# Eight output projection tiles moved into the last head, and the last head's copy, inversion and transfers split in halves over two issuing engines

## The chip, the core and the metric

The kernel runs on one core of one Trainium2 chip. The metric is device time in microseconds (us). Three executions of the kernel before took 399.95, 400.23 and 400.28 us, median 400.23. The profile is that of one further execution.

## What is computed

One transformer layer on 2048 tokens of 256 values, in f32: a layer norm, attention with 16 heads of 16 values, in which a query sees 717 of the 2048 keys (the first 205 and the last 512), and a mixture of eight experts of which each token uses one. Cut to what matters here:

```
xn = layernorm(x)
q, k, v = rope(xn Wq + bq), rope(xn Wk + bk), xn Wv + bv       # 16 heads of 16
attn = softmax(q k^T / 4 over the 717 kept keys)
out  = (attn v).reshape(2048, 256)
y    = x + (out Wo + bo) + weight * down_e(silu(gate_e(xn)) * up_e(xn))
```

The change touches only the last head and the product `out Wo`.

## The kernel before

The program is written out by hand, engine by engine, with semaphores between the engines. After layer norm, projections and experts come the 16 heads. In a head, TensorE makes 24 score units (`S`): for each of six chunks of keys (128, 77, 128, 128, 128, 128) and each of four blocks of 512 queries one bank of PSUM is filled, by four matmuls of 32 columns side by side (line 725, three for the chunk of 77). The banks 4, 5 and 6 take turns, so that unit u waits until ScalarE has finished the exponential of unit u-3. ScalarE takes each unit through the exponential (line 1297). When the four units of a chunk are through, TensorE multiplies them with v (`P`, line 703, four matmuls of 32 columns, f32), accumulating in bank 7. Between them TensorE makes in each head sixteen tiles of the next heads' row maxima (`M`, line 646), which VectorE reduces out of the banks 0 to 3. The string `ORDER` sets how S, M and P follow each other. In the last head (h = 15) there are no further heads, and its sixteen places `M` are empty.

The tail. The heads' outputs go as rows to DRAM, and come back as `attnT`, 128 rows (heads 0 to 7, m = 0) and 128 rows (heads 8 to 15, m = 1); the softmax sums take the same way, are inverted, and come back as `recips`. VectorE multiplies the two (`divide`, line 1131). Heads 0 to 7 are divided before the last head is half done; heads 8 to 13 near its end. Head 15 skips DRAM: ScalarE copies bank 7 to `o_st` (line 1288), SyncE issues four transfers of its rows to `attnT` (line 415), VectorE inverts the whole copy, sums and all, into `last_recip` (line 1151), SyncE issues four transfers of the inverted sums to `recips` (line 419), and VectorE makes four multiplications for the 32 rows of heads 14 and 15.

The output projection (line 762) has 16 tiles of 128 tokens, each the sum of an m = 0 and an m = 1 matmul of 256 columns. It uses all eight banks, two tiles each. TensorE makes all sixteen with m = 0 and then all sixteen with m = 1. After each pair VectorE adds the residual (line 1161), and SyncE stores 256 KB (line 425). A queue stands behind each engine's program order: SyncE's DMAs are issued one after another, and what waits holds what follows.

## Time and profile before

| | us |
|---|---|
| median of three runs | 400.23 |
| the profiled execution | 404.71 |
| its span, first to last instruction | 402.9 |
| TensorE busy | 372.3 |
| VectorE busy | 322.7 |
| ScalarE busy | 270.1 |

The span is 1.8 us shorter than the profiled execution's own time. Start times in what follows are counted from the start of the span. In the timeline, instructions of one line that follow each other are merged into one row: the second number is the time from the first one's start to the last one's end, and the number in brackets is idle time of the engine before the row, with what ended it. The row of an f32 matmul counts two records for each instruction of the program.

### The profile page before, as it was taken

Reading aid. Unit: us, or ns where it says so; the run is one execution under the profiler, and the core shown is the slowest. Engines: PE = TensorE matmul, PEld = TensorE weight load, DVE = VectorE, ACT = ScalarE, POOL = GpSimd, SP = SyncE. Lnnn points to the kernel's source line nnn. Section 1 sums busy time; section 2 is a strip of 40 time slices with the busy share of each in tenths; the row PEclk is TensorE's granted clock in tenths of the full one; section 3 lists DMA queues with packets and bytes.
Section 4 is the critical chain, followed back from the end, with each engine's and each line's share of the span. In section 5 each row is a group of like instructions: output and inputs, shape, how many; then the busy total and the mean of one; then the engine's idle time right before and its main releaser. Section 6 shows DMA issues by size and latency. Waiting matters only on the chain.

```text
span 402.9 us, 12243 instructions
## 1 busy us (share of the span) xinstructions
PE 372.3 (92%) x4646; PEld 193.2 (48%) x4646; DVE 322.7 (80%) x549; ACT 270.1 (67%) x537; POOL 63.9 (16%) x82
## 2 busy tenths in 40 slices
PE   0889988898999999999999999999999999998896
PEld 0556555565674544444444443444444444542265
DVE  5859598777766888888898888988898888984566
ACT  2614564544445887787877878778887888888920
POOL 5005242332200030321303213030000000000000
PEclk9999998999999999999999999999999999999999
DMA  7999346544513030321303213032021121255726
GB/s 234 407 419 174 113 125 205 166 137 139 132 42 95 15 96 5 97 55 45 91 10 98 58 40 96 8 93 55 19 70 42 33 65 27 52 154 104 144 52 209
DMA packets 30920, 42.53 MB, mean 106 GB/s; under 512 B 10724, under 2 KB 25700, under 8 KB 30048
## 3 DMA queue, kind: packets, MB, share of 16 engines
q1 hardware_dynamic: 29000, 36.71, 31.7%
q0 software_dynamic: 1872, 5.11, 4.9%
q8 instruction: 37, 0.61, 0.6%
q14 instruction: 11, 0.09, 0.1%
HBM read 27.75 MB, written 13.67 MB: 103 GB/s over the span
## 4 chain that ended last, share of the span: by engine, by line
PE 80%; DVE 10%; issue 4%; ACT 3%; DMA 1%; SPq 0%; DVEq 0%; ACTq 0%
PE ps L725 20%; PE ps L703 18%; PE ps L646 18%; PE ps L594 6%; PE ps L607 4%; PE ps L762 3%; PE ps L545 3%; DVE mx L1013 3%; PE ps L632 1%; DMA x_sb<-x_in 1%; PE ps L534 1%; PE ps L507 1%; PE ps L501 1%; PE ps L580 1%; PE ps L653 1%
## 5 line engine op out<-in xcount | busy, mean ns | idle before, releaser
L1013 DVE TENSOR_REDUCE mx<-ps 128x1 f32<-128x717 f32 x232 | 198.6, 899 | 30.9 <-PE ps L646 30.7
L725 PE MATMUL ps<-q_op,k_op 98*32 98x512 bf16 (+1 forms) x1472 | 128.8, 381 | 2.5 <-ACT wqk L1297 0.7
L1297 ACT ACTIVATE probs<-ps 128x512 f32<-128x512 f32 x192 | 103.1, 598 | 18.2 <-PE ps L725 16.5
L646 PE MATMUL ps<-k_op,q_op 96*32 96x512 bf16 (+1 forms) x1856 | 111.1, 315 | 0.4 <-DVE mx L1013 0.3
L646 PEld LDWEIGHTS ps<-k_op,q_op 96*32 96x32 bf16 x1856 | 50.6, 96 | 56.2 <-issue 25.7
L725 PEld LDWEIGHTS ps<-q_op,k_op 98*32 98x32 bf16 (+1 forms) x1472 | 42.0, 95 | 65.5 <-ACT probs L1297 14.9
L703 PE MATMUL ps<-probs,v_op 128*32 128x512 f32 x384 | 50.6, 595 | 0.2 <-ACT o_st L1288 0.2
L1297 ACT ACTIVATE dn<-ps 77x512 f32<-77x512 f32 x64 | 34.8, 595 | 10.9 <-PE ps L725 10.9
L1297 ACT ACTIVATE gu<-ps 128x512 f32<-128x512 f32 x64 | 34.5, 598 | 9.1 <-PE ps L725 9.1
L1297 ACT ACTIVATE wqk<-ps 128x512 f32<-128x512 f32 x64 | 33.5, 599 | 8.1 <-PE ps L725 8.1
L454 POOL COPY v_op<-v_all 128x192 f32<-128x192 f32 x16 | 5.7, 361 | 199.4 <-PE ps L703 199.4
L448 POOL DMA_INDIRECT o_st<-sorted_rows,token_of x23 | 25.1, 1089 | 75.4 <-PE ps L580 46.9
L594 PE MATMUL ps<-gu,probs 128*128 x92 | 32.4, 476 | 4.7 <-ACT probs L1227 4.7
L1007 DVE TENSOR_REDUCE mx<-ps 128x1 f32<-128x717 f32 x24 | 21.7, 903 | 6.7 <-PE ps L632 6.4
L594 PEld LDWEIGHTS ps<-gu,probs 128*128 128x128 f32 x92 | 16.1, 193 | 11.9 <-issue 7.2
L545 PE MATMUL ps<-xnT,wqk 128*128 128x512 f32 (+1 forms) x48 | 19.7, 550 | 0.0
L1045 DVE SCALAR_TENSOR_TENSOR probs<-probs,ps 128x176 f32<-128x176 f32 x23 | 7.6, 330 | 13.2 <-ACT probs L1246 13.2
L703 PE MATMUL ps<-dn,v_op 77*32 77x512 f32 x128 | 17.0, 591 | 0.0
L703 PE MATMUL ps<-gu,v_op 128*32 128x512 f32 x128 | 16.5, 592 | 0.2 <-ACT gu L1297 0.2
L703 PE MATMUL ps<-wqk,v_op 128*32 128x512 f32 x128 | 16.5, 592 | 0.0
L501 PE MATMUL ps<-const,xn 128*128 128x128 f32 x32 | 5.9, 353 | 11.2 <-DVE xn L813 11.2
L1246 ACT ACTIVATE probs<-ps 128x176 f32<-128x176 f32 x23 | 7.2, 315 | 13.3 <-PE ps L594 13.3
(127 smaller groups left out, 377.7 us busy)
## 6 DMA issues: line engine op xcount, KB each, us to landing
q_parts<-parts SPq DMA_DIRECT2D x12, 256.0 KB
sorted_results<-ys SPq DMA_DIRECT2D x23, 128.0 KB
q_op<-q_parts SPq DMA_DIRECT2D x15, 192.0 KB
gu<-gu_in SPq DMA_DIRECT2D x1, 2816.0 KB
tab<-tab_in SPq DMA_DIRECT2D x1, 2048.0 KB, 11.8
sorted_rows<-xn SPq DMA_DIRECT2D x4, 512.0 KB, 7.4
out<-x_sb SPq DMA_DIRECT2D x8, 256.0 KB, 2.4
q_op<-q_parts SPq DMA_DIRECT2D x15, 128.0 KB
```

The source lines that it names most:

```text
L448: pool.indirect_dma_start(out=xs[t % XR], out_offset=None, in_=xn_dram, in_offset=bass.IndirectOffsetOnAxis(ap=token_of[:, t:t + 1], axis= ...
L501: ins = pe.transpose(bank(b)[:, 256 * m + P * j:256 * m + P * j + P], xn[:, 2 * pair + j, P * m:P * m + P], ident)
L545: ins = pe.matmul(proj_bank(u, odd), wqk[:, is_q, HID * m + P * odd:HID * m + P * odd + P], xnT[:, m, t0:t0 + n], start=m == 0, stop=m == ...
L594: ins = pe.matmul(bank(b)[:, 0:2 * I], xsT[b][:, P * m:P * m + P], gu[:, bass.ds(e * (HC * 2 * I) + 2 * I * m, 2 * I)], start=m == 0, stop ...
L607: ins = pe.matmul(bank(4 + b)[:, 0:HID], hidT[b][:, P * m:P * m + P], dn[:, bass.ds(e * (2 * HID) + HID * m, HID)], start=m == 0, stop=m == 1)
L646: ins = pe.matmul(ps[r:r + CW, at + c0:at + c0 + n], q_op[slot][0:KR, P * t + r:P * t + r + CW], k_op[slot][0:KR, c0:c0 + n], start=True, ...
L703: ins = pe.matmul(bank(7)[VW * b:VW * b + VW, :], v_op[slot][0:rows, VW * c:VW * c + VW], prob[c][0:rows, QB * b:QB * b + QB], start=c == ...
L725: ins = pe.matmul(bank(4 + u % RING)[r:r + w, :], k_op[k][:, c0 + r:c0 + r + w], q_op[k][:, QB * b:QB * b + QB], start=True, stop=True)
L762: ins = pe.matmul(ps[:, HID * t:HID * t + HID], attnT[:, m, P * t:P * t + P], wo[:, HID * m:HID * m + HID], start=m == 0 and t % 2 == 0, s ...
L1007: dve.tensor_reduce(mx[:, h, t:t + 1], ps[:, EARLY_MAX:EARLY_MAX + NK], AX.X, ALU.max).then_inc(max_reduced, 1)
L1013: dve.tensor_reduce(mx[:, slot, t:t + 1], ps[:, at:at + NK], AX.X, ALU.max).then_inc(max_reduced, 1)
L1297: act.activation(prob[c][0:rows, QB * b:QB * b + QB], bank(4 + u % RING)[0:rows, :], ACT.Exp, scale=SCALE).then_inc(exp_done, 1)
```

## The change

Four things are moved or split.

1. The m = 0 matmuls of the first eight output tiles (t = 0 to 7) go into the last head, at its places `M` number 6 to 13 (counted from 0). There each is cut into four matmuls of 32 columns, side by side.
2. ScalarE copies bank 7 in two halves of 256 columns, and VectorE inverts each half on its own.
3. ScalarE itself issues the four transfers of the head's rows, and the four transfers of the second half's inverted sums; SyncE issues the four of the first half's.
4. The divisions of heads 14 and 15 are eight of 256 columns. The pairs of output tiles are taken in the order 0, 2, 4, 6, 1, 3, 5, 7 (`PAIRS`), first halves of the four query blocks first; the last four divisions stand between VectorE's first additions.

```diff
+EARLY_OUT = 4 * 2
+OUT_SLOTS = {6 + n: n for n in range(EARLY_OUT)}
+PAIRS = [2 * b + half for half in range(2) for b in range(NQB)]
...
+        def load_last_recip(engine, half, b):
+            c0 = QB // 2 * half
+            engine.dma_start(recips[P - DH:P, HC - 1, QB * b + c0:QB * b + c0 + QB // 2],
+                             last_recip[VW * b + DH:VW * b + 2 * DH, c0:c0 + QB // 2]
+                             ).then_inc(last_recip_in[NQB * half + b], 16)
...
-            sp.wait_ge(o_copied, HEADS)
-            for b in range(NQB):
-                sp.dma_start(attnT[P - DH:P, HC - 1, QB * b:QB * b + QB],
-                             o_st[0][VW * b:VW * b + DH, :]).then_inc(last_in[b], 16)
             sp.wait_ge(last_inverted, 1)
             for b in range(NQB):
-                sp.dma_start(recips[P - DH:P, HC - 1, QB * b:QB * b + QB],
-                             last_recip[VW * b + DH:VW * b + 2 * DH, :]).then_inc(last_in[b], 16)
+                load_last_recip(sp, 0, b)
...
+                        if h == HEADS - 1 and j in OUT_SLOTS:
+                            if OUT_SLOTS[j] == 0:
+                                pe.wait_ge(wo_in, 16)
+                                pe.wait_ge(neg_copied, HEADS)
+                                pe.wait_ge(max_reduced, HEADS * NT)
+                            for r in range(0, P, CW):
+                                out_tile(OUT_SLOTS[j], 0, r, CW)
...
+            pe.wait_ge(exp_done, HEADS * UNITS)
+            for t in range(EARLY_OUT, NT):
+                if t == NT - 2:
+                    pe.wait_ge(last_copied, 2)
+                out_tile(t, 0)
+            for n, pair in enumerate(PAIRS):
+                pe.wait_ge(attn_ready, NQB + n + 1)
+                for t in (2 * pair, 2 * pair + 1):
+                    ins = out_tile(t, 1)
+                ins.then_inc(out_proj, 1)
...
-            dve.reciprocal(last_recip[:], o_st[0][:]).then_inc(last_inverted, 1)
+            for half in range(2):
+                dve.wait_ge(last_copied, half + 1)
+                cols = slice(QB // 2 * half, QB // 2 * half + QB // 2)
+                dve.reciprocal(last_recip[:, cols], o_st[0][:, cols]).then_inc(last_inverted, 1)
             dve.wait_ge(attn_in[2], 32)
-            for b in range(NQB):
-                dve.wait_ge(last_in[b], 32)
-                divide(1, P - 2 * DH, P, b, attn_ready)
             dve.wait_ge(y_added, NT)
...
+            for n in range(NQB):
+                divide_last(n)
+            for n, pair in enumerate(PAIRS):
+                if n < NQB:
+                    divide_last(NQB + n)
+                dve.wait_ge(out_proj, n + 1)
                 both = x_sb[:, 2 * pair:2 * pair + 2, :].rearrange("p t d -> p (t d)")
                 dve.tensor_tensor(both, bank(pair), both, ALU.add).then_inc(out_ready, 1)
...
-            copy_o(HEADS - 1, 0)
+            act.wait_ge(pv_done, HEADS * NCH)
+            act.wait_ge(o_stored, (HEADS - 1) * (16 * NQB))
+            for half in range(2):
+                cols = slice(QB // 2 * half, QB // 2 * half + QB // 2)
+                act.copy(o_st[0][:, cols], bank(7)[:, cols]).then_inc(last_copied, 1)
+            act.wait_ge(last_copied, 2)
+            for b in range(NQB):
+                act.dma_start(attnT[P - DH:P, HC - 1, QB * b:QB * b + QB],
+                              o_st[0][VW * b:VW * b + DH, :]).then_inc(last_o_in[b], 16)
+            act.wait_ge(last_inverted, 2)
+            for b in range(NQB):
+                load_last_recip(act, 1, b)
```

TensorE's program in the last head before, from its product of the second chunk with v (`dn,v_op`) to the output projection (`wo,xnT`):

```order
L703 MATMUL ps<-probs,v_op 32x512 x4
L725 MATMUL ps<-q_op,k_op 32x512 x12
L703 MATMUL ps<-dn,v_op 32x512 x4
L725 MATMUL ps<-q_op,k_op 32x512 x20
L703 MATMUL ps<-probs,v_op 32x512 x4
L725 MATMUL ps<-q_op,k_op 32x512 x16
L703 MATMUL ps<-probs,v_op 32x512 x4
L725 MATMUL ps<-q_op,k_op 32x512 x16
L703 MATMUL ps<-wqk,v_op 32x512 x4
L703 MATMUL ps<-gu,v_op 32x512 x4
L762 MATMUL ps<-wo,xnT 128x256 x32
```

The same place in the changed kernel, from the first moved tiles on (line 718 is the output tile, 739 the score units, 710 the product with v):

```order
L739 MATMUL ps<-q_op,k_op 32x512 x4
L718 MATMUL ps<-wo,xnT 32x256 x8
L739 MATMUL ps<-q_op,k_op 32x512 x8
L710 MATMUL ps<-dn,v_op 32x512 x4
L739 MATMUL ps<-q_op,k_op 32x512 x4
L718 MATMUL ps<-wo,xnT 32x256 x4
L739 MATMUL ps<-q_op,k_op 32x512 x4
L718 MATMUL ps<-wo,xnT 32x256 x4
L739 MATMUL ps<-q_op,k_op 32x512 x12
L718 MATMUL ps<-wo,xnT 32x256 x4
L710 MATMUL ps<-probs,v_op 32x512 x4
L718 MATMUL ps<-wo,xnT 32x256 x4
```

Two tiles now stand between the ninth and the tenth score unit, two between the units of the next group, and one on each side of a product with v; after these rows there are one more between score units, and one ahead of the next product. 24 full-width matmuls are left at the end, of 32.

VectorE's last instructions before (line 1151 inverts, 1131 divides, 1161 adds the residual; in brackets the semaphores that each waits for):

```order
L1151 RECIPROCAL o_st<-o_st 128x512 [waits o_stored,o_copied]
L1131 TENSOR_TENSOR xnT<-xnT,tab 32x512 [waits last_in0,attn_in2]
L1131 TENSOR_TENSOR xnT<-xnT,tab 32x512 [waits last_in1]
L1131 TENSOR_TENSOR xnT<-xnT,tab 32x512 [waits last_in2]
L1131 TENSOR_TENSOR xnT<-xnT,tab 32x512 [waits last_in3]
L1161 TENSOR_TENSOR x_sb<-ps,x_sb 128x512 [waits out_proj,y_added]
L1161 TENSOR_TENSOR x_sb<-ps,x_sb 128x512 [waits out_proj] x7
```

And in the changed kernel, from the first division on (1174 divides, 1184 adds):

```order
L1174 TENSOR_TENSOR xnT<-xnT,tab 32x256 [waits last_o_in0,last_recip_in0,y_added,attn_in2]
L1174 TENSOR_TENSOR xnT<-xnT,tab 32x256 [waits last_recip_in1,last_o_in1]
L1174 TENSOR_TENSOR xnT<-xnT,tab 32x256 [waits last_recip_in2,last_o_in2]
L1174 TENSOR_TENSOR xnT<-xnT,tab 32x256 [waits last_recip_in3,last_o_in3]
L1174 TENSOR_TENSOR xnT<-xnT,tab 32x256 [waits last_recip_in4,last_o_in0]
L1184 TENSOR_TENSOR x_sb<-ps,x_sb 128x512 [waits out_proj]
L1174 TENSOR_TENSOR xnT<-xnT,tab 32x256 [waits last_recip_in5,last_o_in1]
L1184 TENSOR_TENSOR x_sb<-ps,x_sb 128x512 [waits out_proj]
L1174 TENSOR_TENSOR xnT<-xnT,tab 32x256 [waits last_recip_in6,last_o_in2]
L1184 TENSOR_TENSOR x_sb<-ps,x_sb 128x512 [waits out_proj]
L1174 TENSOR_TENSOR xnT<-xnT,tab 32x256 [waits last_recip_in7,last_o_in3]
L1184 TENSOR_TENSOR x_sb<-ps,x_sb 128x512 [waits out_proj] x5
```

There are now five divisions ahead of the first addition, and one ahead of each of the next three.

## Rows read from the trace of the kernel before

**Rows 1.** The page: busy time, share of the span and instructions of two engines

```profile
PE 372.3 (92%) x4646; PEld 193.2 (48%) x4646; DVE 322.7 (80%) x549; ACT 270.1 (67%) x537; POOL 63.9 (16%) x82
```

**Rows 2.** Chain of waits, 370 to 403 us: start us, us, what

```profile
381.18 0.86 PE ps L703 x8
...
384.49 1.07 PE ps L703 x8
385.56 14.03 PE ps L762 x64
...
399.61 0.69 DVE x_sb L1161
```

**Rows 3.** Timeline of TensorE's matmuls in the last head: start us, us, instructions

```profile
370.56 0.83 PE L725 MATMUL ps<-q_op,k_op 98*32 98x512 bf16 x12
...
375.36 0.91 PE L725 MATMUL ps<-q_op,k_op 98*32 98x512 bf16 x12
376.10 1.03 PE L703 MATMUL ps<-dn,v_op 77*32 77x512 f32 x8
...
378.77 1.03 PE L703 MATMUL ps<-probs,v_op 128*32 128x512 f32 x8
...
380.78 0.40 PE L725 MATMUL ps<-q_op,k_op 98*32 98x512 bf16 x4 [0.33 <-ACT wqk L1297]
381.01 1.03 PE L703 MATMUL ps<-probs,v_op 128*32 128x512 f32 x8
381.87 0.82 PE L725 MATMUL ps<-q_op,k_op 98*32 98x512 bf16 x12
```

**Rows 4.** Timeline of ScalarE, last head

```profile
382.37 2.06 ACT L1297 ACTIVATE gu<-ps 128x512 f32<-128x512 f32 x4 [0.18 <-PE ps L725]
```

**Rows 5.** Timeline of all engines, the tail

```profile
385.62 0.58 ACT L1288 COPY o_st<-ps 128x512 f32<-128x512 f32 x1 [1.19 <-PE ps L703]
386.24 2.48 SPq L415 DMA_DIRECT2D xnT<-o_st  x4
386.24 3.35 DVE L1151 RECIPROCAL o_st<-o_st 128x512 f32<-128x512 f32 x1 [0.99 <-ACT o_st L1288]
389.62 2.41 SPq L419 DMA_DIRECT2D tab<-o_st  x4
391.63 2.51 DVE L1131 TENSOR_TENSOR xnT<-xnT,tab 32x512 f32<-32x512 f32 x4 [2.03 <-DMA tab<-o_st]
394.17 2.68 DVE L1161 TENSOR_TENSOR x_sb<-ps,x_sb 128x512 f32<-128x512 f32 x4
394.89 5.81 SPq L425 DMA_DIRECT2D out<-x_sb  x8
```

**Rows 6.** Groups of instructions by line and form: busy us, mean ns, idle before

```profile
L762 PE MATMUL ps<-wo,xnT 128*128 128x256 f32 x64 | 14.1, 381 | 0.0
L1260 ACT COPY ys<-ps 128x256 f32<-128x256 f32 x23 | 8.6, 375 | 10.7 <-PE ps L607 9.2 <-issue 1.5
L1102 DVE RECIPROCAL recip_c<-sum_c 128x16 f32<-128x16 f32 x15 | 3.7, 244 | 9.2 <-DMA sum_c<-softmax_sums 9.2
L980 DVE TENSOR_TENSOR v_all<-ps,bvo 128x256 f32<-128x256 f32 x5 | 1.8, 412 | 0.0
```

**Rows 7.** Busy time in stretches: us, engines, granted clock, DMA share, GB/s

```profile
395.00:396.00 1.00, 1.00 (x7) 0.87 (x6) 1.00 (x2) 0.00 (x0) 0.00 (x0) 1.00 0.14 48
396.00:397.00 1.00, 1.00 (x6) 0.90 (x5) 0.74 (x2) 0.00 (x0) 0.00 (x0) 1.00 1.05 339
...
401.00:402.00 1.00, 0.00 (x0) 0.00 (x0) 0.00 (x0) 0.00 (x0) 0.00 (x0) 1.00 0.97 330
402.00:403.00 1.00, 0.00 (x0) 0.00 (x0) 0.00 (x0) 0.00 (x0) 0.00 (x0) 0.68 0.04 11
```

**Rows 8.** Line 419, its DMAs, from issue to landing

```profile
DMA to landing us min/median/max: 1.9/2.0/2.0
```

**Rows 9.** Line 425, the stores of the output, from issue to landing

```profile
DMA to landing us min/median/max: 2.2/2.4/2.6
```

More of the change, by code:

```diff
@@ L228, in layer @@
         attn_in = [sem(f"attn_in{n}") for n in range(3)]
-        last_in = [sem(f"last_in{b}") for b in range(NQB)]
+        last_copied = sem("last_copied")
+        last_o_in = [sem(f"last_o_in{b}") for b in range(NQB)]
+        last_recip_in = [sem(f"last_recip_in{n}") for n in range(2 * NQB)]
         last_inverted = sem("last_inverted")
@@ L411, in _ @@
             load_attn(HEADS - 2, HEADS - 1, attn_in[2])
-            sp.wait_ge(o_copied, HEADS)
-            for b in range(NQB):
-                sp.dma_start(attnT[P - DH:P, HC - 1, QB * b:QB * b + QB],
-                             o_st[0][VW * b:VW * b + DH, :]).then_inc(last_in[b], 16)
             sp.wait_ge(last_inverted, 1)
             for b in range(NQB):
-                sp.dma_start(recips[P - DH:P, HC - 1, QB * b:QB * b + QB],
-                             last_recip[VW * b + DH:VW * b + 2 * DH, :]).then_inc(last_in[b], 16)
+                load_last_recip(sp, 0, b)
             ov = out_d.rearrange("(t p) d -> p t d", p=P)
-            for pair in range(NT // 2):
-                sp.wait_ge(out_ready, pair + 1)
+            for n, pair in enumerate(PAIRS):
+                sp.wait_ge(out_ready, n + 1)
                 sp.dma_start(ov[:, 2 * pair:2 * pair + 2, :], x_sb[:, 2 * pair:2 * pair + 2, :]
@@ L706, in pv, with out_tile @@
                 ins.then_inc(pv_done, 1)
+            def out_tile(t, m, r=0, w=P):
+                pe.wait_ge(attn_ready, NQB if m else t // 4 + 1)
+                return pe.matmul(ps[r:r + w, HID * t:HID * t + HID], attnT[:, m, P * t + r:P * t + r + w],
+                                 wo[:, HID * m:HID * m + HID], start=m == 0 and t % 2 == 0,
+                                 stop=m == HC - 1, skip_group_check=True)
             def head_step(h, k, first=False, rest_of_next=True, start_after=True):
@@ L755, in _ @@
             pv(15, NCH - 1, 0)
-            def out_tile(t, m):
-                pe.wait_ge(attn_ready, NQB * m + t // 4 + 1)
-                ins = pe.matmul(ps[:, HID * t:HID * t + HID], attnT[:, m, P * t:P * t + P],
-                                wo[:, HID * m:HID * m + HID], start=m == 0 and t % 2 == 0,
-                                stop=m == HC - 1, skip_group_check=True)
-                if m == HC - 1 and t % 2 == 1:
-                    ins.then_inc(out_proj, 1)
-            pe.wait_ge(wo_in, 16)
-            pe.wait_ge(neg_copied, HEADS)
-            for m in range(HC):
-                for t in range(NT):
-                    if m == 0 and t == NT // 2:
-                        pe.wait_ge(exp_done, HEADS * UNITS)
-                        pe.wait_ge(o_copied, HEADS)
-                    out_tile(t, m)
+            pe.wait_ge(exp_done, HEADS * UNITS)
[8 more added lines that the diff above has]
+                ins.then_inc(out_proj, 1)
         @block.vector
@@ L1148, in _, with divide_last @@
                 divide(1, 0, P - 2 * DH, b)
-            dve.wait_ge(o_copied, HEADS)
             dve.wait_ge(o_stored, 16 * NQB * (HEADS - 2))
-            dve.reciprocal(last_recip[:], o_st[0][:]).then_inc(last_inverted, 1)
+            for half in range(2):
+                dve.wait_ge(last_copied, half + 1)
+                cols = slice(QB // 2 * half, QB // 2 * half + QB // 2)
+                dve.reciprocal(last_recip[:, cols], o_st[0][:, cols]).then_inc(last_inverted, 1)
             dve.wait_ge(attn_in[2], 32)
-            for b in range(NQB):
-                dve.wait_ge(last_in[b], 32)
-                divide(1, P - 2 * DH, P, b, attn_ready)
             dve.wait_ge(y_added, NT)
-            for pair in range(NT // 2):
-                dve.wait_ge(out_proj, pair + 1)
+            rows = slice(P - 2 * DH, P)
+            def divide_last(n):
+                dve.wait_ge(last_o_in[n % NQB], 16)
+                dve.wait_ge(last_recip_in[n], 16)
+                cols = slice(2 * P * PAIRS[n], 2 * P * PAIRS[n] + 2 * P)
+                dve.tensor_tensor(attnT[rows, 1, cols], attnT[rows, 1, cols], recips[rows, 1, cols], ALU.mult
+                                  ).then_inc(attn_ready, 1)
+            for n in range(NQB):
+                divide_last(n)
+            for n, pair in enumerate(PAIRS):
+                if n < NQB:
+                    divide_last(NQB + n)
+                dve.wait_ge(out_proj, n + 1)
                 both = x_sb[:, 2 * pair:2 * pair + 2, :].rearrange("p t d -> p (t d)")
```

## The prediction

> **What bounds the kernel now.** I read the page first: TensorE is busy for 92% of the span, ScalarE for 67% [rows 1]. Those are averages over stages, and the change touches only the last head and the tail, so I went to the chain of waits from 370 us on. It has two parts. In the last head it goes to and fro between TensorE and ScalarE; a product with v at 381.18 is one of its pieces [rows 2], and the timelines show each of the two waiting for the other, TensorE 0.33 us for an exponential at 380.78, ScalarE 0.18 for a score unit at 382.37 [rows 3, 4]. From 384.49 us on it is TensorE alone: the last product with v, 64 records of the output projection without a gap until 399.6, and one addition [rows 2]. The last head's transfers are not in that chain: the divisions run from 391.63 to 394.14 [rows 5], and TensorE reaches the m = 1 tiles at about 385.6 + 32 x 0.217 = 392.5, when the first of them is done.
>
> The view of stretches shows a second bound at the same place. From 396 to 402 us the DMA engines are full, at 330 to 340 GB/s; the 0.14 in the stretch before puts their start at 395.9, and the next to nothing in the last one their end at 402.05 [rows 7]. Eight stores of 262 KB took 6.15 us, 0.77 each. So the end of the kernel is the larger of two: the first store's data plus 6.15, and the last store's issue plus its own way. The last store is issued when the addition that starts at 399.61 ends (400.3), and lands 2.2 to 2.6 us later [rows 2, 9]. Both give 402.1 for the last byte. Whoever wants to gain in the tail must start the first stores earlier and not leave gaps between them.
>
> **Step 1: eight tiles in the last head.** An m = 0 tile is two records. 64 records take 14.03 us, and one lasts 0.38 [rows 2, 6], so they follow each other after (14.03 - 0.38) / 63 = 0.217 us, and a tile costs 0.43 us. No row shows its new form, four quarters of 32 x 256 in f32. The nearest one is the product with v, four quarters of 32 x 512 in f32: from 381.01 to 381.87, 0.86 us [rows 3]; with half the columns 0.43. From below: the bf16 score unit, four quarters, (0.82 - 0.38) / 2 = 0.22 us [rows 3], if a quarter needed one pass; from above 0.86, if the quarters shared nothing of the shorter length. I take 0.43, since the product with v has the same type, the same width and two passes.
>
> So 8 x 0.43 = 3.46 us leave the tail and enter the head. What hides them there is TensorE's idle time. The first moved tile stands behind the score unit that starts at 375.36, the last one ahead of the product that starts at 381.01 [rows 3]. From 375.36 to 381.87, 6.51 us, TensorE does twelve score units (12 x 0.22 = 2.6) and three products with v (3 x 0.86 = 2.6) [rows 3]. 1.3 us are idle. At least 3.46 - 1.3 = 2.1 us cannot be hidden, and ScalarE has little slack: the score unit at 381.87 lets its exponential start at 382.37, 0.50 later, and ScalarE had already been idle for 0.18 [rows 3, 4].
>
> How much of the 1.3 us is used I worked out by walking the program: each score unit starts when TensorE is free and 0.05 us after the exponential three units back has ended; an exponential starts 0.50 after its unit or 0.48 to 0.49 after the one before, and lasts 0.60; three of the four gaps in 2.06 us give (2.06 - 0.60) / 3 = 0.49 [rows 4]. Without the tiles the walk hits every start in rows 3 within 0.06 us. With them TensorE is idle twice for 0.08 before the unit that was at 381.87, which moves to 384.1. After it nothing is moved, and the rest of the head keeps its shape. The last product with v goes from 384.49 to 386.74: D = 2.25 us. With 0.22 us for a tile the same walk gives D = 1.0, with 0.50 it gives 2.65, with 0.86 it gives 5.5. The three tiles that stand directly before or after a product with v (places 10, 11, 13) cost their whole 0.43 each; only those between score units that wait for ScalarE (9 and 12) cost nothing alone.
>
> **Step 2: copy and inversion in halves.** Times from here are in the frame of before; D is added at the end. The copy starts at 385.62. Half of it is 0.375 us (a copy of 256 columns, rows 6) instead of 0.58. The reciprocal of 16 columns takes 0.244 and that of 512 takes 3.35 [rows 5, 6], 6.26 ns a column, so 256 take 1.75 us. The first half starts at 386.03 and ends at 387.78, where before the whole ended at 389.59: 1.8 us earlier.
>
> **Step 3: transfers.** SyncE issues its four at 387.8. Four issues take 2.41 us [rows 5], 0.6 us apart, and each lands 1.9 to 2.0 later [rows 8]. I keep both for the half-size transfers; from below an issue could cost half, 0.3. They land at 389.75, 390.3, 390.95 and 391.55. ScalarE's rows are issued from about 386.3, if it issues as SyncE does; they land by 390.2 and have 1.4 us to spare. Its second halves are issued at about 389.5, land from 391.45 and have 0.5 us to spare. No row shows ScalarE issuing a DMA; that is bounded by nothing (if it issues faster) and by the 0.6 us of SyncE's issue added to each of its own four if the two queues share what issues them, 2.4 us.
>
> Four issues in a row take longer (2.41 us) than one transfer takes to land (2.0) [rows 5, 8]. The Trainium skill, DMA: Bandwidth & Descriptors, section "Issuing engines are not separate DMA queues", says that issuing from several engines saves only the issue time, "which is usually small relative to the DMA itself". By that rule the split over two engines would be worth next to nothing; by the rows it is not small here, since four further issues on SyncE would have ended at 388.8, after the first half's inversion at 387.8, and the split is worth 1.0 us. The sum goes by the rows.
>
> **Step 4: VectorE.** A division of 512 columns follows the one before after 0.61 us, (2.51 - 0.68) / 3 [rows 5]. One of 256 costs between 0.31 (half) and 0.41 (a tensor_tensor of 256 columns, rows 6); I take 0.34. An addition behind a division starts only when that has ended: 391.63 + 2.51 = 394.14, and the addition at 394.17 [rows 5], so there a switch costs 0.1 more. Divisions 0 to 3 follow the transfers, the last at 391.63; division 4 at 391.97; the first addition at 392.35, its store 0.72 later (394.17 to 394.89, rows 5) at 393.07. Before it was 394.89: 1.8 us earlier. But then an addition with a division ahead of it comes only every 0.61 + 0.34 = 0.95 us, or 1.05 with the switch, while a store needs 0.77 us. The first three gaps leave the DMA engines idle for 3 x 0.18 to 3 x 0.28, 0.55 to 0.85 us, and then the stores run at 0.77. What is left of 1.8 is 0.95 to 1.25 us; I take 1.1. TensorE is no bound there: from 390.3 it makes a pair in 0.86 and would be through at 397.2.
>
> **The sum.** D - 1.1 = 2.25 - 1.1 = +1.15 us. The profiled execution would go from 404.71 (span 402.9 and 1.8 around it) to 405.9. The median of the runs is 4.5 us below the profiled one; I carry the difference over: 400.23 + 1.15 = 401.4 us. The forecast's own range is 400.9 to 401.9, for D between 2.1 and 2.5 and a tail gain of 0.8 to 1.3.
>
> **The rivals.**
>
> Hidden: TensorE's idle time takes the tiles up, and the transfers' gain comes through. The place is the last head, the price D; with D below 1.1 the kernel gets faster. For it: over the whole last head, 13.9 us from 370.56 to 384.49, TensorE has 24 score units and six products with v, 24 x 0.22 + 6 x 0.86 = 10.4, and is idle for 3.5 us, as much as the tiles need [rows 2, 3]. Against it: only 1.3 of that lie where the tiles stand, by rows 3. With D = 0.2 it would be 399.3 us. This is the case on the other side.
>
> Half hidden: a tile of four quarters costs between 0.22 and 0.35 us, D between 1.0 and 1.75, and the time is 400.1 to 400.9 us, no change that can be told. For it speaks only that the form is new; against it that the f32 records of both line 703 and line 762 need two passes.
>
> Crowded queues: SyncE's four issues lie beside ScalarE's last two, and ScalarE's second four beside SyncE's last. If two issues at a time each take their 0.6 us one after the other, the first halves come 0.6 us later and the second halves 0.6 to 1.2, VectorE's queue holds the additions behind them, and the time is 402.0 to 402.6. For it: 16 short rows a transfer cost 0.6 us to issue [rows 5], which is time of whatever writes descriptors. Against: SyncE's own transfers land 2.0 us after their issue although the next are being issued by then [rows 8]. (The Trainium skill's page DMA: Bandwidth & Descriptors, in the section named above, has DMAs of several engines run on the same 16 DMA engines and interleave; whether they also share the issue, no run here shows.)
>
> Unshared quarters: 0.86 us for a tile, D = 5.5, 404.6 us.
>
> **How the numbers follow.** Forecast (401.4) 0.50; half hidden (400.5) 0.18; hidden (399.3) 0.12; crowded queues (402.3) 0.16; unshared quarters (404.6) 0.04. What a measurement of this kernel can tell from no change is 0.2%, 0.8 us, so from 399.4 to 401.0. Slower has the forecast but for its lower edge, and the two last cases, 0.64; same has half hidden and that edge, 0.24; faster 0.12. The range 400.1 to 402.5 takes in half hidden and crowded queues, and leaves out the hidden case, the unshared quarters and a little more.
>
> **What would show it.** In the changed kernel's trace: the last product with v starts at about 386.7 (step 1; near 384.5 is the hidden rival), TensorE's idle time between 375.4 and 384.1 is nearly gone, and ScalarE waits for TensorE in its place. A moved tile takes 0.43 us to the next instruction. Two reciprocals of 1.75 us (step 2). ScalarE's issues 0.6 us apart and landings of 2.0 (step 3; longer ones are the crowded rival). The first addition at 394.6, stores with gaps between the first four, and the DMA engines full only from the fourth on (step 4). The forecast is wrong if the last product with v starts before 385.6.

## The result, and the profile after

The change made the kernel slower. Over 20 runs each, the kernel before had a median of 401.33 us and the changed one 402.51 us; run against run the ratio is 1.0044, with a 95% interval of 1.0026 to 1.0061, which on 400 us is 1.0 to 2.4 us, with 1.8 in the middle. The forecast was slower, by 1.15 us. That shift lies in the interval, but the time itself was put at 401.4 with a range up to 402.5, and 402.51 is just outside of it. Two things did that. The forecast started from 400.23, the median of three runs, and over 20 runs the kernel before has 401.33, 1.1 us more. And one term of the sum, the gain in the tail, was put too high. Either alone would have left the time inside the range: 400.23 + 1.8 is 402.0, and 401.33 + 1.15 is 402.48. The first is no matter of the mechanism; the second is what the experiments are about.

The runs of one kernel spread over several us (398.7 to 403.8 before, 400.8 to 404.5 after), and the last head starts between 365 and 371 us in the traces, whatever is changed behind it. So the traces are compared by their **last stretch**: from the first score unit of the last head to the end of the span. It is 32.35 us in the trace of before (370.56 to 402.91) and 34.65 us in the first trace of the changed kernel (368.05 to 402.70), 2.3 us longer. It falls into two parts at the last product with v: 13.93 and 18.42 us before, 16.26 and 18.39 us after.

TensorE in the last head, timeline of the changed kernel (line 718 is the output tile, 710 the product with v, 739 the score units):

```profile
375.23 0.43 PE L739 MATMUL ps<-q_op,k_op 98*32 98x512 bf16 x4
375.45 0.64 PE L718 MATMUL ps<-wo,xnT 128*32 128x256 f32 x8
375.88 0.43 PE L739 MATMUL ps<-q_op,k_op 98*32 98x512 bf16 x4
376.10 0.65 PE L718 MATMUL ps<-wo,xnT 128*32 128x256 f32 x8
...
377.72 1.03 PE L710 MATMUL ps<-probs,v_op 128*32 128x512 f32 x8
378.58 0.60 PE L718 MATMUL ps<-wo,xnT 128*32 128x256 f32 x8
379.01 0.39 PE L739 MATMUL ps<-q_op,k_op 98*32 98x512 bf16 x4
379.23 0.60 PE L718 MATMUL ps<-wo,xnT 128*32 128x256 f32 x8
...
384.31 1.07 PE L710 MATMUL ps<-gu,v_op 128*32 128x512 f32 x8 [0.20 <-ACT gu L1320]
```

From the start of a tile to the next instruction it is 0.43 us (375.45 to 375.88, 378.58 to 379.01), as worked out from the product with v [rows 3]. Between the first moved tile and 381.69, where TensorE waited for ScalarE before, it now works without a hole, and ScalarE waits for it:

```profile
379.51 2.17 ACT L1320 ACTIVATE wqk<-ps 128x512 f32<-128x512 f32 x4 [0.94 <-PE ps L739]
382.19 2.06 ACT L1320 ACTIVATE gu<-ps 128x512 f32<-128x512 f32 x4 [0.51 <-PE ps L739]
```

The numbers in brackets are ScalarE's idle time ahead of a chunk of four units. Before, the second was 0.18 [rows 4].

The tail, timeline of the changed kernel (1165 inverts, 1174 divides, 1184 adds, 432 stores; 266 and 1339 are the last head's transfers):

```profile
385.44 0.65 ACT L1336 COPY o_st<-ps 128x256 f32<-128x256 f32 x2 [1.19 <-PE ps L710]
385.91 3.37 DVE L1165 RECIPROCAL o_st<-o_st 128x256 f32<-128x256 f32 x2 [2.73 <-ACT o_st L1336]
386.12 2.51 ACTq L1339 DMA_DIRECT2D xnT<-o_st  x4
387.69 2.49 SPq L266 DMA_DIRECT2D tab<-o_st  x4
389.31 3.49 ACTq L266 DMA_DIRECT2D tab<-o_st  x4
389.68 0.42 DVE L1174 TENSOR_TENSOR xnT<-xnT,tab 32x256 f32<-32x256 f32 x1 [0.41 <-DMA tab<-o_st]
...
392.32 0.69 DVE L1184 TENSOR_TENSOR x_sb<-ps,x_sb 128x512 f32<-128x512 f32 x1
393.04 6.80 SPq L432 DMA_DIRECT2D out<-x_sb  x8
393.55 0.42 DVE L1174 TENSOR_TENSOR xnT<-xnT,tab 32x256 f32<-32x256 f32 x1 [0.54 <-DMA tab<-o_st]
394.00 0.69 DVE L1184 TENSOR_TENSOR x_sb<-ps,x_sb 128x512 f32<-128x512 f32 x1
394.73 0.42 DVE L1174 TENSOR_TENSOR xnT<-xnT,tab 32x256 f32<-32x256 f32 x1
395.18 0.69 DVE L1184 TENSOR_TENSOR x_sb<-ps,x_sb 128x512 f32<-128x512 f32 x1
```

Counted from the last product with v, the first addition starts at 8.0 us (392.32 - 384.31) instead of 9.7 (394.17 - 384.49, rows 2 and 5). That part of the new tail works. But the next additions come 1.7 and 1.2 us apart, where a store needs 0.77. One gap holds a wait of 0.54 for a transfer; the other none. The stretches show what the DMA engines make of it (us, engines, granted clock, DMA share, GB/s):

```profile
394.00:395.00 1.00, 1.00 (x6) 0.88 (x5) 0.97 (x2) 0.00 (x0) 0.00 (x0) 1.00 0.74 256
395.00:396.00 1.00, 1.00 (x6) 0.89 (x5) 0.94 (x3) 0.00 (x0) 0.00 (x0) 1.00 0.33 114
396.00:397.00 1.00, 1.00 (x6) 0.64 (x5) 0.97 (x3) 0.00 (x0) 0.00 (x0) 1.00 0.63 214
397.00:398.00 1.00, 0.51 (x3) 0.10 (x1) 1.00 (x3) 0.00 (x0) 0.00 (x0) 1.00 0.61 204
398.00:399.00 1.00, 0.00 (x0) 0.00 (x0) 1.00 (x3) 0.00 (x0) 0.00 (x0) 1.00 1.02 336
```

Before, they were full from the first store on [rows 7]; now they are busy for 0.33 to 0.74 of each of four microseconds. VectorE's busy share beside it is 0.94 to 1.00: it is the bound in these.

The late transfer is one of ScalarE's four of inverted sums. The view of line 266 has its DMAs, from issue to landing, in this trace:

```profile
L266 ACTq DMA_DIRECT2D tab<-o_st x4: 514/615/1655, 389.3 to 391.1; - x4
DMA to landing us min/median/max: 1.7/1.9/3.6
```

One of ScalarE's issues lasted 1.66 us in place of 0.6. Its second transfer landed after 3.6 us in place of 1.9, and its third and fourth after 3.1 and 2.9. In the DMA view from 389 to 393.5 us stands the row

```profile
q8 instruction: 1, 0.02, 1.6%
```

a transfer of instructions of 16 KB, which held one of the DMA engines for 1.1 us at that time.

### The profile page after: what moved, and what is told of

The parts are those of the page before. It is cut to its first block, busy times and chain, and to the rows that moved or that the text cites. A ratio compares the mean times of both kernels' runs of the same rounds, so it can differ in the third digit from the quotient of the medians.

```text
span 402.7 us, 12366 instructions
## 1 busy us (share of the span) xinstructions
PE 370.7 (92%) x4694; PEld 193.3 (48%) x4694; DVE 322.9 (80%) x554; ACT 270.6 (67%) x538; POOL 64.6 (16%) x82
## 4 chain that ended last, share of the span: by engine, by line
PE 76%; DVE 9%; DMA 6%; issue 3%; ACT 2%; SPq 2%; DVEq 0%; ACTq 0%
PE ps L739 20%; PE ps L710 19%; PE ps L653 17%; PE ps L601 5%; PE ps L614 4%; PE ps L552 3%; DMA softmax_sums<-o_st 2%; PE ps L639 1%; DMA x_sb<-x_in 1%; PE ps L514 1%; PE ps L541 1%; PE ps L508 1%; DMA tab<-o_st 1%; PE ps L718 1%; DVE o_st L1165 1%
## 5 line engine op out<-in xcount | busy, mean ns | idle before, releaser
L653 PEld LDWEIGHTS ps<-k_op,q_op 96*32 96x32 bf16 x1856 | 51.8, 96 | 54.0 <-issue 22.8
L718 PE MATMUL ps<-wo,xnT 128*32 128x256 f32 (+1 forms) x112 | 15.9, 382 | 1.1 <-DVE xnT L1174 1.1
```

Of the source, the lines that this page charges most:

```text
L653: ins = pe.matmul(ps[r:r + CW, at + c0:at + c0 + n], q_op[slot][0:KR, P * t + r:P * t + r + CW], k_op[slot][0:KR, c0:c0 + n], start=True, ...
L718: return pe.matmul(ps[r:r + w, HID * t:HID * t + HID], attnT[:, m, P * t + r:P * t + r + w], wo[:, HID * m:HID * m + HID], start=m == 0 an ...
```

## The experiments

"Ratio" is the time against that of the kernel before, run beside it on the same chip; experiments 9 and 10 are one execution each and have none. "Last product" is the start of the last product with v, counted from the first score unit of the last head; "tail" is from there to the end of the span.

| kernel | ratio (95%) | last product | tail | stretch |
|---|---|---|---|---|
| before | | 13.93 | 18.42 | 32.35 |
| the changed kernel, first trace | 1.0044 (1.0026 to 1.0061) | 16.26 | 18.39 | 34.65 |
| 1 the changed kernel again | 1.0056 (1.0031 to 1.0081) | 16.25 | 17.92 | 34.17 |
| 2 tiles only | 1.0073 (1.0048 to 1.0098) | 17.52 | 18.91 | 36.43 |
| 3 tail only | 1.0022 (0.9998 to 1.0046) | 13.94 | 18.96 | 32.89 |
| 4 tiles in TensorE's waits | 1.0002 (0.9977 to 1.0027) | 14.48 | 17.86 | 32.34 |
| 5 all transfers by SyncE | 1.0085 (1.0060 to 1.0111) | 16.26 | 19.10 | 35.36 |
| 6 as 4, divisions first | 0.9994 (0.9968 to 1.0020) | 14.49 | 17.84 | 32.33 |
| 7 as 4, GpSimd divides | 0.9984 (0.9962 to 1.0006) | 14.49 | 16.64 | 31.14 |
| 8 as 7, row maxima earlier | 0.9962 (0.9943 to 0.9982) | 14.48 | 16.62 | 31.10 |
| 9 as 6, needless 32-row work | not measured | 14.48 | 19.12 | 33.60 |
| 10 as 6, needless 128-row work | not measured | 14.48 | 18.34 | 32.82 |
| 11 before, row maxima earlier | 1.0007 (0.9988 to 1.0025) | 13.93 | 18.40 | 32.33 |
| 12 as 8, six tiles | 0.9968 (0.9947 to 0.9989) | 13.98 | 16.64 | 30.62 |

**1. The changed kernel again.** No edit.

> The changed kernel once more, for a second trace. The measure of all runs here is the last stretch, from the first score unit of the last head to the end of the span: 32.35 us in the kernel before, 34.65 in the first trace of the changed one. Two parts: last product with v 13.94 and 16.26 us into the stretch, and from there to the end 18.41 and 18.38. If the late landing of ScalarE's second transfer of inverted sums (3.6 us after its issue, beside 1.7 to 2.0 for the others) is a property of the program, it comes again at the same transfer, and the last stretch is 34.5 to 34.8. If it was chance, all eight land within 2.0, VectorE's first gap shrinks from 1.68 to about 1.2 and the stretch is 34.1 to 34.3.

The last product stands at 16.25 again. The late landing did not come back. Line 266 in this trace:

```profile
L266 ACTq DMA_DIRECT2D tab<-o_st x4: 515/611/619, 387.7 to 389.6; - x4
DMA to landing us min/median/max: 1.7/1.8/1.9
```

No transfer of instructions lies among the last head's transfers here, and the tail is 17.92, 0.47 shorter. That the one caused the other is inferred from their falling together, but not in this pair alone. A transfer of instructions starts between the first issue and the last landing of the last head's transfers in four of the fourteen traces (the first of the changed kernel, 2, 5 and 7), and in all four some of them land late, after 2.7 to 3.8 us; no landing in the ten others took more than 2.4. In the trace of experiment 7 it is the same three transfers again:

```profile
L268 ACTq DMA_DIRECT2D tab<-o_st x4: 514/615/1511, 385.3 to 387.2; - x4
DMA to landing us min/median/max: 1.7/1.9/3.5
```

What is shown is that the delay comes in some executions and not in others of one program, and that without it the new tail is worth 0.50 us, not 1.1. The stretch, 34.17, is 1.82 us longer than before; the timed runs allow 1.0 to 2.4 (the first 20) and 1.2 to 3.2 (experiment 1).

**2. Tiles only.** The kernel before, with this in the last head and nothing else of the change:

```
+EARLY_OUT = 4 * 2
+OUT_SLOTS = {6 + n: n for n in range(EARLY_OUT)}
...
+                        if h == HEADS - 1 and j in OUT_SLOTS:
...
+                            for r in range(0, P, CW):
+                                out_tile(OUT_SLOTS[j], 0, r, CW)
...
-                for t in range(NT):
+                for t in range(0 if m else EARLY_OUT, NT):
```

> Only the eight tiles are moved into the last head, at the places of the change; copy, inversion, transfers and divisions are those of before. Theory (TensorE overflows in the head, and in the tail it was only covering the transfers): last product with v at 16.2 to 16.3, the rest of the tail 18.2 to 18.4 as before, since the first addition waits for VectorE's four divisions; the stretch is 34.4 to 34.7, 2.1 to 2.3 us longer than before, the whole slowdown. Rival (the slowdown comes from the new tail): last product near 14 and the stretch 32.0 to 32.6.

The stretch of 36.43 us missed both expectations. Two disturbances sit in this trace. Ahead of the last head TensorE had stood still for 1.9 us, and from 368 on, before the first moved tile, its clock was at half, the lower of its two levels, 1.2 GHz (granted clock in the next to last columns):

```profile
366.00:368.00 2.00, 0.56 (x12) 0.27 (x12) 1.46 (x4) 0.05 (x1) 0.00 (x0) 0.95 0.09 11
368.00:370.00 2.00, 2.00 (x20) 0.49 (x15) 2.00 (x5) 2.00 (x4) 0.00 (x0) 0.50 0.75 213
```

The product with the first chunk came at 5.22 instead of 3.95 for that. From that product to the last one it is 12.30 us, before 9.99: the tiles cost 2.31 us, as in the changed kernel. And SyncE's four issues of rows took 3.79 us instead of 2.48, of which 0.5 us reached the end; a transfer of instructions lies beside them too. The ratio, 1.9 to 3.9 us, holds 2.3. The rival, that the slowdown is of the new tail's making, is out: there is no new tail here.

**3. Tail only.** The changed kernel with no moved tile (TensorE's three waits ahead of the first tile go behind the head with it):

```
-EARLY_OUT = 4 * 2
+EARLY_OUT = 0
...
```

> Only the tail is changed (halves, two issuing engines, eight divisions); all 16 tiles with m = 0 stay behind the head. Theory: last product with v at 13.94; TensorE ends its 16 tiles 8.0 us later, the first addition is 9.1 after the product instead of 9.7, then 1.17 us for each of three additions with a division before them, and the stores from the fourth on run at 0.77: 18.4 to 18.9 to the end, stretch 32.4 to 32.9, 0 to 0.5 longer than before. Rival (the new tail is worth its 1.1 us and only the overflow ate it): 31.2 to 31.6.

Last product 13.94, first addition 9.07 us later, the next three 1.18, 1.17 and 1.18 apart, tail 18.96: in its one trace half a microsecond worse than the old tail, at the upper edge of what was expected. The timed runs do not tell it from the kernel before (0.9998 to 1.0046). The new tail needs the moved tiles, since without them TensorE reaches the first pair no earlier than 8 us after the product; and even the 0.6 us that the first store gains is lost in the three gaps behind it.

**4. Tiles in TensorE's waits.** The changed kernel, with the same eight tiles ahead of other instructions:

```
-OUT_SLOTS = {6 + n: n for n in range(EARLY_OUT)}
+OUT_AT = {("S", 6): (0,), ("S", 7): (1,), ("S", 13): (2, 3), ("S", 17): (4,), ("S", 19): (5,),
+          ("S", 22): (6,), ("P", 4): (7,)}
...
```

`("S", 6): (0,)` puts tile 0 ahead of score unit number 6, `("P", 4): (7,)` puts tile 7 ahead of product number 4, both counted from 0.

> The changed kernel with its eight tiles at other places in the last head, where the trace of before shows TensorE waiting for ScalarE: before the score units 6, 7, 13 (two tiles), 17, 19, 22 and before the fifth product with v. Theory: by the same walk as in the prediction the last product with v moves by 0.5 us only, to 14.45; the tail is that of the changed kernel, 18.0 to 18.4; stretch 32.4 to 32.9. Rival (each tile costs ScalarE its 0.43 wherever it stands, for example through PSUM or the sequencer): last product at 16 or later, stretch 34.4 or more.

Last product at 14.48, against 14.45 from the walk: the same eight tiles cost 0.55 us in place of 2.32. So the price was one of place. The stretch is that of the kernel before, 32.34, and the ratio is 1.0002 (0.9977 to 1.0027). The rival needed 16 or more.

**5. All transfers by SyncE.** The changed kernel with ScalarE's eight transfers moved into SyncE's program:

```
+            sp.wait_ge(last_copied, 2)
+            for b in range(NQB):
+                sp.dma_start(attnT[P - DH:P, HC - 1, QB * b:QB * b + QB], ...)
+            for half in range(2):
+                sp.wait_ge(last_inverted, half + 1)
+                for b in range(NQB):
+                    load_last_recip(sp, half, b)
```

> The changed kernel, with all twelve transfers of the last head issued by SyncE (four of rows, then the four of each half's inverted sums), none by ScalarE. Last product with v as in the changed kernel, 16.25 us into the stretch. If an issue takes 0.6 us and they follow each other (what the traces show), the row transfers hold SyncE until 20.6, and the first half's sums are issued at 20.6 instead of 19.64: the divisions and the first addition come 0.95 later, at 25.2, the second half's sums land from 25.0 to 26.9 and no longer just in time, and the tail is 18.9 to 19.2 us instead of 17.92, the stretch 35.1 to 35.5. If the issue is small beside the transfer and one engine does as well as two, the tail stays at 17.9 to 18.1.

The tail is 19.10 us, 1.18 longer. SyncE's queue (start us, us to the end of the last issue):

```profile
386.01 2.48 SPq L427 DMA_DIRECT2D xnT<-o_st  x4
388.54 5.01 SPq L266 DMA_DIRECT2D tab<-o_st  x8
394.16 6.29 SPq L437 DMA_DIRECT2D out<-x_sb  x8
```

Twelve issues follow each other 0.63 us apart. The first inverted sums leave 0.94 us later than with two engines. For transfers of 16 and 32 KB that land 1.8 to 2.0 us after their issue, twelve issues in a row are what counts. The rule quoted in the prediction from the Trainium skill, DMA: Bandwidth & Descriptors, section "Issuing engines are not separate DMA queues", calls the issue usually small; this trace does not agree, with 0.63 us for an issue against 1.8 to 2.0 to the landing. (The last of the twelve landed after 3.1 us, beside a transfer of instructions; its division came later than that in any case, behind VectorE's additions.) And the crowded rival of the prediction is out, although the 402.51 us that were measured lie where it had put the time: with ScalarE issuing beside SyncE, each kept its 0.6 us (experiment 1: 586 to 597 ns and 515 to 619 ns).

**6. Divisions first.** As 4, with VectorE's eight divisions ahead of its first addition:

```
-            for n in range(NQB):
+            for n in range(2 * NQB):
                 divide_last(n)
             for n, pair in enumerate(PAIRS):
-                if n < NQB:
-                    divide_last(NQB + n)
```

> The kernel with the tiles in TensorE's waits (last product with v at 14.5), and all eight divisions of the last two heads ahead of VectorE's first addition. Theory (VectorE's mixed sequence, 1.17 us for an addition with a division before it, starves the stores, which need 0.77): the first addition waits for the eighth division, whose sums land about 8.8 us after the last product, so it starts at 9.2 instead of 8.0; from there the additions are 0.61 apart, the stores run back to back, and the tail is 9.2 + 0.7 + 1.0 + 6.2 + 0.3 = 17.4 us instead of 17.9; stretch 31.9. Rival (the order on VectorE is not what holds the stores): the tail grows by the 1.2 us by which the first store is later, to 19.0.

The timeline of VectorE:

```profile
388.71 1.91 DVE L1176 TENSOR_TENSOR xnT<-xnT,tab 32x256 f32<-32x256 f32 x5 [0.22 <-DMA tab<-o_st]
390.66 4.88 DVE L1184 TENSOR_TENSOR x_sb<-ps,x_sb 128x512 f32<-128x512 f32 x8
```

The first addition comes 1.16 us later than in 4, the eighth ends 0.57 earlier, and the tail is the same, 17.84 against 17.86. So the gaps between the additions were worth 1.2 us: as much as the later start takes is given back. The number in the expectation, 17.4, was wrong since it gave the last store 0.3 us from its last byte to the end of the span; it is 0.8. With that, the fourth store's issue plus 5.65 us (1.0 to its first data, five stores at 0.77, and 0.8) gives the end of experiments 1, 3, 4 and 5 within 0.1 us.

**7. GpSimd divides.** As 4, with the four divisions of the second halves on GpSimd; TensorE's last four pairs wait for these instead of VectorE's:

```
+            pool.wait_ge(attn_in[2], 32)
+            for n in range(NQB, 2 * NQB):
+                pool.wait_ge(last_o_in[n % NQB], 16)
+                pool.wait_ge(last_recip_in[n], 16)
...
+                pool.tensor_tensor(attnT[rows, 1, cols], attnT[rows, 1, cols], recips[rows, 1, cols], ALU.mult
+                                   ).then_inc(pool_divided, 1)
```

> The kernel with the tiles in TensorE's waits, and GpSimd makes the four divisions of the second halves, so that VectorE's additions follow each other. Theory: first addition 7.7 us after the last product with v (behind the fourth division, not the fifth), the next at the pace of TensorE (0.86) or the stores (0.77); stores begin at 8.4, their data at 9.4, 6.2 us of data: tail 15.9 to 16.5 us instead of 17.9, stretch 30.4 to 31.0, 1.4 to 2.0 us shorter than in the kernel before. A GpSimd multiplication of 32 x 256 should last 0.75 us at most (128 x 256 took 0.744). Rival: GpSimd's divisions are slow or late, TensorE waits for them at its fifth pair, and the tail stays above 17.5.

Tail 16.64, stretch 31.14, 1.2 us shorter than before the change; slightly short of the expectation. The ratio, 0.9984 (0.9962 to 1.0006), leaves it open whether this kernel alone is faster. The late landings of this trace did not reach the end: experiment 8, without them, has the same tail. GpSimd's first division lay beside VectorE's fourth, and that one took 0.70 us (0.69 and 0.68 in experiments 8 and 12, 0.42 in the traces where GpSimd does nothing there):

```profile
387.24 0.72 POOL L502 TENSOR_TENSOR xnT<-xnT,tab 32x256 f32<-32x256 f32 x1 [48.96 <-DMA tab<-o_st]
...
386.93 0.42 DVE L1189 TENSOR_TENSOR xnT<-xnT,tab 32x256 f32<-32x256 f32 x1 [0.17 <-DMA tab<-o_st]
387.55 0.70 DVE L1189 TENSOR_TENSOR xnT<-xnT,tab 32x256 f32<-32x256 f32 x1 [0.20 <-DMA tab<-o_st]
```

**8. Row maxima earlier.** As 7; in head 14 SyncE issues `load_neg(15)` ahead of its wait for the sums of head 13:

```
-            head_step(14, 2, load=False)
+            head_step(14, 2, load=False, neg_early=True)
...
```

> As the one with GpSimd's divisions, and in head 14 SyncE issues the transfer of the last head's row maxima before it waits for the softmax sums of head 13 to land, not behind that wait. In five of six traces so far TensorE stood still for 0.5 to 1.9 us ahead of the last head's first score unit, waiting for that transfer, and in one its clock fell to 1.2 GHz behind it. Theory: that wait is gone, and the median is 0.5 to 1.5 us below that of the kernel with GpSimd's divisions; the last stretch keeps its length. Rival: the transfer is held up by what the DMA engines are doing, not by SyncE's order, and nothing changes.

**11. The same edit on the kernel before.**

> The kernel before, with nothing of the change, and SyncE's transfer of the last head's row maxima issued ahead of its wait for the sums of head 13. Theory: the wait ahead of the last head, 0.5 to 1.9 us in the traces and none in the first one, is not of the change's making and costs the kernel before about 0.8 us in its median too; this kernel is 0.3 to 1.2 us faster than before, last stretch 32.3. Rival: the wait comes only with the change, and nothing is gained here.

Experiment 11 does not bear the theory out: the ratio is 1.0007 (0.9988 to 1.0025), so the edit gains at most 0.5 us on the kernel before. A wait of 0.5 us or more is in seven of the eleven traces of kernels that lack the edit, up to 1.9 us long, and in none of the three that have it. But the only trace of the kernel before has 0.1 us of it, and whether its timed executions have more is not known; so the rival, that the wait comes with the change, is not refuted either. Experiment 8 is faster than before clear of the noise (0.9962, 0.9943 to 0.9982), but its distance to 7 is not told apart, and it is not put down to this edit.

**9 and 10. Needless work between the additions.** As 6, with this ahead of the second, third and fourth addition, on 32 rows and on 128:

```
+            idle_rows = slice(P - 2 * DH, P)
...
+                if 0 < n < 4:
+                    dve.tensor_tensor(probs[idle_rows, n - 1, 0:QB // 2], o_st[2][idle_rows, 0:QB // 2],
+                                      o_st[2][idle_rows, QB // 2:QB], ALU.mult)
```

In experiment 10 the slice is `slice(0, P)`. So the two differ in the number of rows and also in where they begin: rows 96 to 127 in experiment 9, as in the divisions, and rows 0 to 127 in 10.

> The kernel with the tiles in TensorE's waits and all divisions ahead of the additions; ahead of the second, third and fourth addition VectorE makes a multiplication that no one needs, of 32 rows x 256 in SBUF, with no semaphore. In the changed kernel an addition with a division before it took 1.17 us (0.72 to the division, 0.45 to the next addition), 0.22 more than 0.61 + 0.34. If the switch between 32 and 128 rows costs that, it is 1.17 here too. If the division's waits or its signal to TensorE cost it, it is 0.95 here.

> The same with the needless multiplications on 128 rows x 256. If the number of rows is what costs, an addition with one of them takes 0.95 us; if the switch between an operand in PSUM and operands in SBUF alone costs it, or anything else that has nothing to do with rows, 1.17.

VectorE with 32 rows, and then with 128:

```profile
388.96 0.69 DVE L1188 TENSOR_TENSOR x_sb<-ps,x_sb 128x512 f32<-128x512 f32 x1
389.68 0.42 DVE L1184 TENSOR_TENSOR probs<-o_st 32x256 f32<-32x256 f32 x1
390.12 0.69 DVE L1188 TENSOR_TENSOR x_sb<-ps,x_sb 128x512 f32<-128x512 f32 x1
```

```profile
390.22 0.69 DVE L1188 TENSOR_TENSOR x_sb<-ps,x_sb 128x512 f32<-128x512 f32 x1
390.82 0.41 DVE L1184 TENSOR_TENSOR probs<-o_st 128x256 f32<-128x256 f32 x1
391.16 0.68 DVE L1188 TENSOR_TENSOR x_sb<-ps,x_sb 128x512 f32<-128x512 f32 x1
```

From addition to addition it is 1.16 us with 32 rows and 0.94 with 128. The work has the same 256 columns, the same 0.42 us and no semaphore. On 128 rows each instruction starts 0.08 before the one ahead has ended; with 32 rows the multiplication starts 0.03 after the addition has ended and the next addition 0.01 after the multiplication. The two switches cost 0.22 us together, about 0.11 each.

The number of rows alone is not what costs it. The trace of the kernel before has VectorE changing from 128 to 32 rows and back, rows 0 to 31, with each instruction starting 0.06 to 0.09 before the one ahead has ended. It also has six additions of one kind in a row, the fourth on 77 rows from row 0 up and the others on 128, all 0.33 us apart:

```profile
347.77 1.72 DVE L1013 TENSOR_REDUCE mx<-ps 128x1 f32<-128x717 f32 x2
349.40 0.20 DVE L1030 COPY neg_row<-ps 32x128 bf16<-32x128 bf16 x1
349.54 0.88 DVE L1013 TENSOR_REDUCE mx<-ps 128x1 f32<-128x717 f32 x1
```

```profile
35.83 2.07 DVE L980 TENSOR_TENSOR v_all<-ps,bvo 128x256 f32<-128x256 f32 x6
```

In all fourteen traces the instructions that lose the 0.1 us at a change of rows, with nothing to wait for, are those that go to rows 96 to 127 or come from them. So it is the beginning of the rows that the traces point at. No run has the same multiplication on 32 rows from row 0 up, so this is inferred.

**12. Six tiles.** As 8, with six moved tiles:

```
-EARLY_OUT = 4 * 2
+EARLY_OUT = 6
...
+OUT_AT = {("S", 6): (0,), ("S", 7): (1,), ("S", 13): (2,), ("S", 17): (3,), ("S", 22): (4,), ("P", 4): (5,)}
```

> The fastest kernel so far (tiles in TensorE's waits, GpSimd's divisions, the earlier transfer), with six tiles moved in place of eight. By the walk the last product with v is at 14.0 instead of 14.48, and the two tiles more behind it fit ahead of the first division, which ends 5.8 us after the product: ten tiles take 1.1 + 10 x 0.43 = 5.4. Stretch 30.6 to 30.8 instead of 31.10, the median 0.2 to 0.6 below. If TensorE is the bound behind the product after all, the stretch is 31.0 or more.

Last product at 13.98, tail 16.64 as in 7 and 8: ten tiles still fit in front of the first division.

```profile
381.14 4.58 PE L731 MATMUL ps<-wo,xnT 128*128 128x256 f32 x20
...
385.53 0.42 DVE L1191 TENSOR_TENSOR xnT<-xnT,tab 32x256 f32<-32x256 f32 x1 [0.41 <-DMA tab<-o_st]
...
386.01 7.17 PE L731 MATMUL ps<-wo,xnT 128*128 128x256 f32 x32 [0.29 <-DVE xnT L1191]
```

TensorE waits only 0.29 us between the ten m = 0 tiles and the m = 1 tiles. This kernel has the shortest stretch, 30.62 us, and the lowest median, 398.99 against 400.49 for the kernel before, run beside it. It beats both kernels, by 0.3% against the one before (0.1 to 0.5); the changed one was not run beside it, but is 0.4 to 0.6% slower than the kernel before. Against experiment 8 the difference is within the noise of the runs.

## Why the prediction was right, and where it was off

The way, slower, and the mechanism were right. Two numbers that went into the time were not, and together they put it outside the range: the tail's gain, which was put at 1.1 us in step 4 and measured 0.50, and the 400.23 us that the sum started from.

**Step 1, the tiles in the head: right.** D was put at 2.25 us, and is 2.31 to 2.32 in the four traces with the tiles at the change's places. A tile costs 0.43 us. Experiment 4 tests the walk where it says something else than counting: the same tiles, other places, 0.5 predicted and 0.55 measured. The hidden rival, which looked at the idle time of the whole head, was refuted by D; with a better placement it would have been nearly right about D (0.55 against its 0.2).

**Step 2: right.** 1.75 and 1.70 us for the two inversions.

**Step 3: right in its main line.** ScalarE issues as SyncE does, 0.6 us each, and the two do not hold each other up. Half-size transfers land 1.7 to 1.9 us after issue. The spare time of 0.5 us for ScalarE's sums was enough in experiment 1 and not in the first trace, where the second of the four landed 1.7 us late. The split over two engines, put at 1.0 us, is worth 0.94 in the issue and 1.18 at the end (experiment 5).

**Step 4, VectorE: the term that was mis-sized.** The tail's gain was put at 1.1 us, from a first addition 7.86 us after the last product and gaps of 0.95 to 1.05. Experiment 1 has it at 8.01, and gaps of 1.17 to 1.18: 0.15 and three times 0.17 over the middle taken, and the gain is 0.50. The prediction saw the 0.1 us ahead of an addition in the trace of before (the end of the last division against the start of the first addition, rows 5), and charged it once a pair, at half weight. It falls due twice, going to the divisions' 32 rows and coming back (experiment 9 against 10). With 1.17 for a gap the sum would have been 2.25 - 0.6 = 1.65 us; the timed runs say 1.8 (1.0 to 2.4) and the traces 1.82.

**The form of the bound: right.** The stores need 0.77 us each and cannot catch up what a gap leaves idle; experiments 3 and 6 show this from both sides.

**The sum's starting value: 1.1 us too low.** The prediction took the median of three runs, 400.23, as the level of the kernel before and gave it no width of its own in the range. Over 20 runs it is 401.33, beside three later sets of 23 to 31 runs 400.49 to 400.74, so three runs did not fix it. How the 1.13 us between 401.38 and 402.51 divide between the two numbers depends on the measure: the medians of the 20 runs differ by only 1.18 us, nearly the forecast's 1.15, which leaves almost all to the starting value; the ratio and the traces say 1.8, which leaves 0.6 to the tail's gain. That the medians come so near to the forecast is luck, since the trace shows the gain at half its size.

**What was not foreseen** is also chance: the late landings beside a transfer of instructions, 0.47 us in one of the changed kernel's two traces.

Two slips in the working change nothing: by its own terms the forecast's own range begins at 401.0, not 400.9 (400.23 + 2.1 - 1.3), and the last store's way of 2.2 to 2.6 us is the one to its landing, 402.5, not to the last byte at 402.1.

## What to carry to other kernels

Work moved into an engine's idle time is nearly free only where that engine waits ahead of the very instruction it is put before (0.55 us for eight tiles against 2.32); walk the program with its waits, since the idle time of the whole stage says nothing. When several producers feed a stream of stores that is itself at its bandwidth, a late first store and a gap between two early ones cost the same, so moving foreign work from between them to ahead of them gave nothing (experiment 6), and giving it to another engine gave 1.2 us (experiment 7). A forecast of a time, and not only of a shift, needs the spread of the kernel before in its range. Where many small transfers must go at once, count their issues before their bytes.

## What the runs showed of the hardware

- VectorE started a 128-row instruction 0.08 us before the end of the one ahead. Going to 32 rows that begin at row 96 it started 0.03 after the end, and coming back 0.01 to 0.03 after: about 0.11 us lost at each switch, in experiment 9 with no semaphore on the multiplication, against none in 10. Changes from 128 to 32 or 77 rows that begin at row 0, and back, cost nothing of this (trace of before).
- ScalarE and SyncE issued DMAs side by side with next to no loss: 0.60 us for ScalarE alone (experiment 1), 0.59 for SyncE alone (experiment 5), and 0.51 to 0.62 for either where both issued (experiment 1).
- A VectorE multiplication of 32 x 256 took 0.68 to 0.70 us beside one of GpSimd, and 0.42 otherwise (experiments 7, 8 and 12).
- A transfer of instructions of 16 KB took 0.9 to 1.5 us on one DMA engine. In the four traces in which one starts among the last head's transfers, landings went from 1.8 to 2.0 us up to 3.1 to 3.8, and in three of them one issue from 0.6 to 1.5 to 1.9 us. It lies at another time in each trace.
- After 1.9 us without a matmul ahead of the last head, the granted clock was 0.50 from 368 to 370 us in experiment 2; in the other traces, with waits up to 1.5 us there, it stayed at 1.00.
